# A local-attention transformer on one core: VectorE makes the rotary tables, and three sample loops are written out

## What is computed

```python
def attn_layer(x, Wqkv, qs, ksc, Wo):
    qkv = x @ Wqkv
    q, k, v = split into 16 heads of 64
    q = l2norm(q) * qs
    k = l2norm(k) * ksc
    cos, sin = (jnp.cos(freqs), jnp.sin(freqs))
    q = q * cos * scale + rotate_half(q) * sin * scale
    inv = 1.0 / scale
    k = k * cos * inv + rotate_half(k) * sin * inv
    out = local_attention(q, k, v)      # windows of 32 keys, own and previous
    return out @ Wo
```

## Time and profile before

| what | value |
|---|---|
| median of 3 runs | 4807.2 us (4794.04 to 4811.34) |
| the profiled execution | 4809.91 us, its span 4808.1 us |
| PE busy | 4411.5 us, 92% of the span |
| DVE busy | 3259.4 us, 68% |
| ACT busy | 2761.8 us, 57% |
| POOL busy | 2215.3 us, 46% |
| mean granted clock of PE | 0.979 |
| second pass, 48 trips | 1390.7 to about 4714 us |

### The profile page before, as it was taken

How to read it: one execution, slowest core, us unless ns; L and a number is a source line. 1 busy time by engine, 2 the same in 40 slices (tenths; PEclk the granted TensorE clock), 3 DMA queues, 4 the chain that set the end, 5 groups by cost and what they waited for, 6 DMA issues and landing times. The chain is left out here.

```text
span 4808.1 us, 174636 instructions
## 1 busy us (share of the span) xinstructions
PE 4411.5 (92%) x67636; PEld 2576.4 (54%) x67636; DVE 3259.4 (68%) x5741; ACT 2761.8 (57%) x5481; POOL 2215.3 (46%) x2020
## 2 busy tenths in 40 slices
PE   7888888888869999999999999999999999999995
PEld 4445444544445555555555555555555555555553
DVE  4545545554547777777777777777777777777772
ACT  4434544443346666666666666666666666666663
POOL 0000000000046666666666666666667666666661
PEclk9999999999899999999999999999999999999997
DMA  1000000000012111211122111211122111221112
GB/s 37 8 6 8 6 6 6 9 6 4 3 50 53 44 46 46 68 47 46 46 56 59 46 46 41 64 50 50 42 60 54 46 47 46 59 55 47 46 46 62
DMA packets 144907, 188.51 MB, mean 39 GB/s; under 512 B 34151, under 2 KB 66298, under 8 KB 144250
## 3 DMA queue, kind: packets, MB, share of 16 engines
q1 hardware_dynamic: 144250, 178.39, 13.7%
HBM read 29.39 MB, written 4.19 MB: 7 GB/s over the span
## 5 line engine op out<-in xcount | busy, mean ns | idle before, releaser
L1336 POOL TENSOR_TENSOR cs<-cs 128x512 f32<-128x512 f32 x768 | 980.6, 1277 | 571.9 <-DVE cs L1647 566.7
L1463 PE MATMUL psum<-wqkv,xw 128*128 128x512 f32 x2304 | 1193.1, 610 | 34.8 <-POOL xw L1373 24.9
L1647 DVE TENSOR_TENSOR cs<-psum,rots 128x1024 f32<-128x1024 f32 x768 | 938.3, 1222 | 299.4 <-PE psum L1463 266.9
L1345 POOL TENSOR_TENSOR qk<-cs,rn 128x512 f32<-128x512 f32 x768 | 777.2, 1044 | 338.2 <-ACT rn L1529 282.8
L1545 ACT ACTIVATE sq<-psum 128x512 f32<-128x512 f32 x768 | 459.3, 598 | 657.8 <-DVE cs L1647 619.7
L1371 POOL MEMSET qTl<- 128x2048 f32 x1 | 1.8, 1805 | 1350.9 <-POOLq L498 1350.9
L1608 DVE TENSOR_REDUCE ss<-sq 128x8 f32<-128x512 f32 x768 | 520.1, 677 | 7.0
L1414 PEld LDWEIGHTS psum<-pT,vw 64*64 64x64 f32 x18624 | 401.2, 135 | 194.3 <-issue 193.7
L1468 PEld LDWEIGHTS psum<-ident,qk 128*128 128x128 f32 x3088 | 354.2, 142 | 270.6 <-issue 152.8
L1468 PE MATMUL psum<-ident,qk 128*128 128x128 f32 x3088 | 448.7, 279 | 51.2 <-DVE state L1681 31.5
L1463 PEld LDWEIGHTS psum<-wqkv,xw 128*128 128x128 f32 x2304 | 369.1, 190 | 198.5 <-issue 172.7
(11 more groups left out here) (205 smaller groups left out, 6977.4 us busy)
## 6 DMA issues: line engine op xcount, KB each, us to landing
vw<-vl SPq DMA_DIRECT2D x768, 128.0 KB, 2.4
vw<-vl SPq DMA_DIRECT2D x672, 64.0 KB, 2.0
wqkv<-in_wqkv SPq DMA_DIRECT2D x42, 256.0 KB, 4.0
wol<-in_wol SPq DMA_DIRECT2D x7, 512.0 KB, 4.0
w1l<-in_w1l SPq DMA_DIRECT2D x7, 341.0 KB
xin<-in_x SPq DMA_DIRECT2D x9, 256.0 KB, 2.8
xr<-in_x SPq DMA_DIRECT2D x8, 256.0 KB, 3.9
sums<-sumout SPq DMA_DIRECT2D x8, 256.0 KB, 2.7
```

What stands on the lines that cost most here:

```text
L1336: summed_rot.done(nc.gpsimd.tensor_tensor(own, own, halves(cs[:, t % 2, j, 1, :])[:, :, ::-1, :], ALU.add), at)
L1345: rotated.done(nc.gpsimd.tensor_tensor(qk[:, j, :].rearrange("p (h c) -> p h c", c=EL), cs[:, t % 2, j, 0, :].rearrange("p (h c) -> p h c" ...
L1463: last = nc.tensor.matmul(ps[:, :], xw[:, t * P:(t + 1) * P], wqkv[:, col:col + BANK], start=True, stop=True)
L1647: parts.done(V.tensor_tensor(cs[:, t % 2, j, :, :].rearrange("p i (h c) -> p i h c", c=EL), twice, by_head, ALU.mult), at)
```

## The change

DVE makes the tables instead of POOL. It makes those of layer 0 before the loop, after a wait for the loaded tables, and those of the next layer in the last sample (s = 7) of each layer, right after its own last use of the old ones (`qk.3.3`); before them stand a wait for its own last reading and a `settle`, an increment of a semaphore. In the last layer they are made once more, for layer 0, and not used. POOL's four multiplications, its wait and its start value of `scaled` are gone; DVE's wait on `scaled` at the head of a trip now asks for 4 (l + 1). Besides, DVE, ACT and POOL no longer have a hardware loop over the samples: as on PE, the 8 bodies stand one behind the other within the loop over the layers.

```diff
@@ def _(pool)
-            pool.sem_inc(scaled, 4)
...
-            pool.wait_ge(rot_loaded, 48)
             with pool.Fori(0, DEPTH) as l:
-
-                parts.wait_before(pool, l * B, pieces[-1])
-                for a in range(2):
-                    for b in (2 * a, 2 * a + 1):
-                        nc.gpsimd.tensor_tensor(
-                            rots[:, b, :, :], rot[:, b, :, :],
-                            qks[:, a, bass.ds(l, 1), :].to_broadcast([P, T, EL]), ALU.mult).then_inc(scaled, 1)
-                with pool.Fori(0, B) as s:
+                for s in range(B):
@@ def _(act)
-                with act.Fori(0, B) as s:
+                for s in range(B):
@@ def _(dve)
+            def scale_tables(l):
+
+                for a in range(2):
+                    for b in (2 * a, 2 * a + 1):
+                        V.tensor_tensor(rots[:, b, :, :], rot[:, b, :, :], qks[:, a, bass.ds(l, 1), :].to_broadcast([P, T, EL]),
+                                        ALU.mult).then_inc(scaled, 1)
...
+            dve.wait_ge(rot_loaded, 48)
+            scale_tables(0)
             with dve.Fori(0, DEPTH) as l:
-                with dve.Fori(0, B) as s:
+                for s in range(B):
                     it = l * B + s
-                    dve.wait_ge(scaled, l * 4 + 8)
+                    dve.wait_ge(scaled, l * 4 + 4)
                     for key in order:
                         read(it, l, s, key)
+                        if s == B - 1 and key == ("qk", *pieces[-1]):
+                            parts.wait(dve, it, pieces[-1])
+                            settle(dve, passed)
+                            scale_tables((l + 1) % DEPTH)
                     chain.end()
```

## The result

The changed kernel takes 4781.2 us (median; 4778.3 to 4783.6), the kernel before beside it 4807.4: the ratio is 0.9947 (95% interval 0.9933 to 0.9962). The profiled execution took 4782.56 us, 27.3 less than that of before; its span is 4780.8 us and its mean clock 0.977.

What follows compares the result with a forecast made beforehand. PE, busy 92% of the span, was taken as the bound, so only its waits cost; boundary gains 2.1 + 2.5 + 2.5 + 1.2 + 1.1 = 9.4 took 4809.9 to 4800.5, median 4798, range 4790 to 4812 us.

Steps and rivals of the forecast that it cites:

- Loops written out: At trip edges of DVE, ACT and POOL: no wait that a branch causes, so nothing gained; cost 0.
- POOL's tables go: At five layer boundaries: 2.78 us of POOL's tables leave the path to DVE's first `cs`; 9.4 us gained in sum.
- The low clock "would be so whatever DVE does", and at two boundaries: At the first and third boundaries: clock 0.50 for 3.4 us after PE's idle, whatever DVE does; gains 1.2 and 1.1.
- The mask at +7.9 with a low clock: At low-clock boundaries: PE reaches the scores' mask +7.8 to +7.9 us after its first matmul, instead of 9.12.
- DVE's jump at about +1.45: At a layer boundary: DVE's jump back lets its first `cs` start 1.45 us after PE's first matmul.
- The tables cost nothing: In a layer's last sample: four tables on DVE, 0.41 us each, 1.65 together, hidden behind ACT's work; cost 0.
- Rival A: Last sample: DVE's tables wait for POOL's addition, second exponential 0.6 us late; 3.6 us of gain gone, 4801.5; chance 0.27.
- Rival B: At layer boundaries: DVE's code after its jump comes as late as the tables did; nothing won, 4807; chance 0.13.
- Rival C: At the attention output's small matmuls: new instruction streams delay PE's, up to 48 x 0.8 = 38 us, 4836; chance 0.1.
- The closing sentence of the prediction: On quiet trips, those away from layer boundaries: the prediction would be wrong altogether if they changed their 68.3 us.

Runs made afterwards that it cites:

- early address: Kernel before, loops kept, plus two one-column copies by DVE that read the same place of the state ahead of the wait for PE: 4790.7 against 4809.3 us.
- the tables alone: Kernel before with the tables moved to DVE; DVE loops over samples 0 to 6, the last written out; ACT and POOL as before: 4792.7 against 4804.1 us.
- a fixed place in the add: Kernel before, loops kept, with DVE's add into `xm` reading sample 1 of the state in every trip: 4801.6 against 4804.1 us.
- its other profile: The changed kernel measured once more, beside the kernel before on the same chip: 4773.2 against 4807.8 us.
- all jumps announced: Changed kernel with a hint at the layer loop's head announcing the jump back on PE, DVE, ACT and POOL: 4765.1 against 4809.3; again 4765.8 against 4807.8 us.
- PE's jump announced: Changed kernel with a hint on PE alone that announces the jump back at the head of its layer loop: 4775.3 against 4809.3 us.

## Why the prediction was wrong

The step that failed is "Loops written out": "DVE, ACT and POOL have no wait at a trip's edge that a branch causes, so nothing is gained there." For the edge and the branch that holds; the loops of ACT and POOL gave nothing that the times can tell, and the kernel with every loop of before and an early address gained 19 us. But I looked at the edge alone. The loop's variable also stands in an address in the middle of the trip, and its register instructions stood between PE's last matmul of the projection and DVE's add, in a place where PE waited for the add. The term that I put at 0 measures 20 us alone (21 with DVE's loop only), and with both parts 0.63 in each of 36 trips. Of the 0.60 by which the place of `xm` in the two trips above moved (44.74 to 44.14), 0.42 are this address. 0.09 are another register instruction ahead of DVE's second `cs` of a trip (3.41 to 3.32 after PE's first matmul; [0.44] and [0.35] of idle time). A last 0.09 comes at POOL's multiplication by the norms. It shows also with the tables alone, where POOL's loop stays, and with ACT's and POOL's loops alone, where the tables stay (the first multiplication at +10.51 or +10.52 instead of +10.60), but not with DVE's loop alone; what it is stays open.

The shortest of the 36 trips between in each profile shows the three terms apart:

| kernel | shortest trip, us |
|---|---|
| before | 68.27 |
| a fixed place in the add | 68.29 |
| the tables alone | 68.19 |
| ACT's and POOL's loops | 68.18 |
| the early address | 67.86 |
| DVE's loop | 67.78 |
| the three loops | 67.69 |
| the changed kernel | 67.69 |

The early address is worth 0.41, the rest of DVE's loop 0.08 to 0.09 more, and POOL's multiplication as much again.

Could the rows have told it? Yes: the idle row of `xm`, 0.46 from PE's end to DVE's start, against 0.04 at the write of the state in the kernel before (PE's `y2` ends at 2085.16, the write starts at 2085.20):

```profile
2082.32 2.84 PE L1499 MATMUL psum<-hf,w2l 114*128 114x512 f32 x6
```
```profile
2085.20 1.52 DVE L1681 SCALAR_TENSOR_TENSOR state<-psum,b2l,xm 64x512 f32 x2 [2.18 <-PE psum L1499]
```

A gap of that kind with "<-PE" behind it is not PE's.

Point by point:

**POOL's tables go**: right in its mechanism. DVE's first `cs` stands at +1.26 to +2.16 in the changed kernel, forecast 1.2 to 2.0. With a full clock the mask was forecast at +7.0 and came at +6.91 to +7.29 with the tables alone. Their sum of 9.4 over five boundaries is there 9.35, with the luck in it that is told above. In the whole change it is 4.1 (0.70, 0.72, 0.55, 1.05 and 1.09), because of the two terms next.

**The low clock "would be so whatever DVE does", and at two boundaries**: wrong in number. It fell at five of five in the changed kernel, at four in its other profile, at one with the tables alone, at none with the fixed place in the add and at none with all jumps announced. Counted over the ten profiles without an announcement, the five in which DVE's loop is written out have 4, 4, 4, 4 and 5 falls, the five in which it is kept 0, 1, 2, 2 and 2. Why, no run shows: PE's idle time is much the same (1.68 to 2.23 in the kernel before, 2.00 to 2.17 in the changed one), and the changed kernel's four and five stand against each other with the same code.

**The mask at +7.9 with a low clock**: too early, it is +8.42 or +8.43 each time in the changed kernel. I had added 4.1 to DVE's second `cs`, the distance that held while DVE was late. Now it is 4.71 (1942.02 to 1946.73), and PE reaches the mask without a wait: the bound is PE's own matmuls and turns at half clock, not DVE.

**DVE's jump at about +1.45**: near enough, +1.26 to +2.16. DVE idles 2.06 at the first boundary of the changed kernel and 2.70 with PE's jump announced, on both sides of the 2.46 of the first pass.

**The tables cost nothing**: right. 0.41 each, as forecast, and hidden, even with the first at 1.13.

**Rival A**: the lock is there, its consequence not. I had let it push the second exponential by 0.6 and all behind it; measured at the write of the state it is 0.

**Rival B** is out: DVE's `cs` never stood later than +2.2 at a boundary. **Rival C** is out: the second instruction queue has 285 packets instead of 79 over the program, and PE's "issue" before L1405 in this kernel is not longer than the one before L1414 was (206.3 us against 210.1, all its instructions counted).

The closing sentence of the prediction, that I would be wrong altogether if quiet trips changed their 68.3 us, named the right place to look.

## What to carry to other kernels

When a loop is written out, or an index becomes a constant, look first at the register instructions that its variable feeds: those that stand behind a wait on the critical path cost their whole length each time (here 0.42 us, 48 times), and a cheap instruction that uses the same address ahead of the wait takes them off the path without unrolling anything. In a timeline such a place shows as a gap between the end of the releaser and the start of the waiter that is larger than at other waits of the same pair of engines. When removing an operand in which an address is computed brings nothing, look whether the next user of the address now computes it.

## What the chip showed that I had not expected

A jump over a long body costs PE 2.00 to 2.17 us of idle time in the changed kernel (1.63 to 2.70 over all profiles without an announcement) and DVE 1.9 to 2.7. An announcement at the head of the loop takes PE's to 0.29 to 0.60 (0.16 to 0.99 over the three profiles with all jumps announced), and DVE's goes on under the write of the state. The Trainium skill, Runtime: NRT & Kernel Launch, section Instruction fetch mechanics, says that a taken branch out of the held pages stalls for a fetch, and from that advises full unrolling. The stall is there as it says, 2.8 to 3.4 us from branch to next instruction on DVE. That it is a fetch no row shows, but it fits that an announcement takes it away. The gain of unrolling, though, came from the address in this kernel, and the stall could be removed with the loop in place.

With all jumps announced, and PE idle for at most 1.0 us there, the clock stayed full at all fifteen boundaries of three profiles. With PE's idle time of 1.6 to 2.7 us it fell to 0.5 at none to five out of five, from kernel to kernel and from run to run, for 3.4 us each; with PE's jump alone announced it fell twice, after waits of 1.7 us ahead of the mask. One fall at a boundary cost 1.1 to 1.5 us at the mask (+8.42 against +6.91 to +7.29 with the tables alone).
